# A graph network's last layer on one core: attention edges and node normalizations in one merged sweep

## What is computed

```python
xl = (x @ Wl + bl).reshape(n, H, C)
xr = (x @ Wr + br).reshape(n, H, C)
e = leaky_relu(xl[src] + xr[dst] + edge_attr @ We, 0.2)
logits = einsum('ehc,hc->eh', e, att)
alpha = softmax of logits over the edges with the same dst
out = segment_sum(alpha[..., None] * xl[src], dst) + bias
z1 = gelu(out) + x
out = layernorm(layernorm(z1) * gamma + beta + x)
```

## Time and profile before

| | us |
|---|---|
| time, median of 3 runs (15389.94 to 15460.77) | 15446.91 |
| span of the profiled execution | 14488.1 |
| of it `gat_edges`, first to last indirect DMA | 11556.0 to 13287.9 |
| of it `gat_nodes`, first addition to the end | 13304.7 to 14488.1 |
| busy in the span: VectorE, ScalarE, GpSimd, TensorE | 7705.7, 4873.1, 9282.4, 5851.2 |

### The profile page before, as it was taken

One profiled execution on the slowest core, in us unless ns is written; L12 is line 12 of the kernel. 1 busy time (PEld: TensorE's weight loads), 2 busy tenths in 40 slices (PEclk: granted clock), 3 DMA queues, 4 the chain that ended last, 5 costly groups with the idle time before them and its releaser, 6 DMA issues. The chain is left out here.

```text
span 14488.1 us, 162751 instructions
## 1 busy us (share of the span) xinstructions
PE 5851.2 (40%) x33264; PEld 4851.5 (33%) x33265; DVE 7705.7 (53%) x16353; ACT 4873.1 (34%) x8868; POOL 9282.4 (64%) x8791
## 2 busy tenths in 40 slices
PE   0000467356725660135634553455245455553000
PEld 0000356346625650024523452345244422221000
DVE  2200367346725679635535773355256544445898
ACT  0000123123312335434434552244146522223666
POOL 5767776577477633477657655774776377776665
PEclk9998678678867885577867776678577777776555
DMA  9201357357725777425624663355256611112333
GB/s 182 41 2 27 115 192 242 100 174 265 257 82 202 257 248 250 157 85 170 224 89 142 216 225 96 121 196 197 72 179 236 204 37 42 44 45 63 134 134 120
DMA packets 1063382, 2125.24 MB, mean 147 GB/s; under 512 B 264966, under 2 KB 576863, under 8 KB 1063288
## 3 DMA queue, kind: packets, MB, share of 16 engines
q1 hardware_dynamic: 421762, 1236.80, 25.6%
q10 hardware_dynamic: 403206, 512.24, 10.7%
q0 software_dynamic: 238336, 375.36, 9.0%
HBM read 1467.05 MB, written 719.11 MB: 151 GB/s over the span
## 5 line engine op out<-in xcount | busy, mean ns | idle before, releaser
L1304 POOL DMA_INDIRECT node_sums<-m_result,m_place x2744 | 3047.3, 1111 | 1027.3 <-issue 723.6
L1335 PE MATMUL m_turn<-k_ident,m_rows 128*128 128x128 f32 x2744 | 595.1, 387 | 2934.9 <-DMA m_rows<-node_rows_b,m_idx 1155.9
L1294 POOL DMA_INDIRECT m_rows<-node_rows_a,m_idx x1176 | 1268.2, 1078 | 471.1 <-issue 342.7
L1335 PEld LDWEIGHTS m_turn<-k_ident,m_rows 128*128 128x128 f32 x2744 | 466.5, 199 | 3036.6 <-issue 2125.7
L1294 POOL DMA_INDIRECT m_rows<-node_rows_b,m_idx x784 | 840.7, 1072 | 314.0 <-issue 224.8
L1391 PE MATMUL m_turn<-k_ident,m_in_y 128*128 128x128 f32 x5488 | 857.5, 302 | 404.3 <-ACT m_nodeT L1418 257.5
L1391 PEld LDWEIGHTS m_turn<-k_ident,m_in_y 128*128 128x128 f32 x5488 | 691.2, 156 | 532.6 <-ACT m_nodeT L1418 326.6
L1774 DVE SCALAR_TENSOR_TENSOR m_acc<-m_out,m_scales,m_res_b 128x128 f32<-128x128 f32 (+1 forms) x2352 | 634.7, 341 | 393.3 <-PE m_out L1403 322.9
L1403 PE MATMUL m_out<-k_sage_r,m_nodeT 128*128 128x128 f32 x3136 | 556.5, 351 | 584.7 <-DVE m_z L1886 571.2
L1761 DVE SCALAR_TENSOR_TENSOR m_res_b<-m_in_sums,m_scales,m_res_b 128x128 f32<-128x128 f32 (+1 forms) x2352 | 631.7, 342 | 292.3 <-DMA m_in_sums<-node_sums 292.0
L1418 ACT ACTIVATE m_nodeT<-m_turn 128x512 f32<-128x512 f32 x980 | 545.4, 596 | 701.4 <-PE m_turn L1391 697.6
(11 more groups left out here) (256 smaller groups left out, 17668.6 us busy)
## 6 DMA issues: line engine op xcount, KB each, us to landing
m_in_sums<-node_sums SPq DMA_DIRECT2D x679, 512.0 KB
m_in_y<-node_rows_a SPq DMA_DIRECT2D x291, 512.0 KB
node_rows_a<-m_y ACTq DMA_DIRECT2D x194, 512.0 KB
m_in_x<-in_x_dram SPq DMA_DIRECT2D x194, 512.0 KB
m_in_y<-node_rows_b SPq DMA_DIRECT2D x194, 512.0 KB
node_rows_a<-m_o ACTq DMA_DIRECT2D x194, 512.0 KB
m_w_all<-edge_w SPq DMA_DIRECT2D x147, 512.0 KB, 4.9
node_sums<-deg_zero ACTq DMA_DIRECT2D x98, 512.0 KB
```

Of the source, the lines that this page charges most:

```text
L1294: pool.indirect_dma_start(self.rows[b][:, t, :], None, self.table[:, :], bass.IndirectOffsetOnAxis(self.idx[b][:, t:t + 1], 0)).then_inc(s ...
L1304: pool.indirect_dma_start(self.dram["node_sums"][:, :], bass.IndirectOffsetOnAxis(self.place[b][:, t:t + 1], 0), self.result[b][:, t, :], ...
L1335: mm = pe.transpose(self.turn_ps[i % 2][:, n * P:(n + 1) * P], self.rows[i // 2][:, H * (i % 2) + n, :], self.k["ident"][:, :])
```

## The change

`gat_edges` and `gat_nodes` become one phase, `gat_conv` ("g8", tiles `g_...`): every engine walks a pair of edge chunks and then the node pairs that are ready (`edges_and_nodes`). The scatter goes to a table of its own, `gat_sums`, filled in the degrees phase with the layer's bias row instead of zeros (98 further DMAs of 512 KB behind the present ones); the rows of nodes with edges get the bias through `blb`, the bias of the values. So the addition L1118 goes. The product with gamma moves from GpSimd to VectorE. The addition of beta to x stays on GpSimd (`shift_x`), with a tile `xb` of its own for the result, and GpSimd walks the node pairs for it. The roots of both norms are taken by ScalarE (Sqrt) instead of Newton steps. Tiles have two copies, one for each chunk of a pair, and each chunk has its own norm tiles for 8 row slots. Waits with values of the loop counter are all kept positive by grants at the start.

```diff
+                dve.tensor_tensor(k["blb"][:, :], k["bl"][:, :], k["gat_bc"][:, :], ALU.add).then_inc(misc, 1)
...
+                act.wait_ge(constants_set, 4)
                 with act.Fori(0, sh.node_chunks) as c:
                     act.dma_start(dram["node_sums"][bass.ds(c * CH, CH), :].rearrange("(p j) f -> p j f", j=T),
                                   zero[:, :, :]).then_inc(zeroed, 16)
-                act.wait_ge(zeroed, 16 * sh.node_chunks)
+                with act.Fori(0, sh.node_chunks) as c:
+                    act.dma_start(dram["gat_sums"][bass.ds(c * CH, CH), :].rearrange("(p j) f -> p j f", j=T),
+                                  bias_rows[:, :, :]).then_inc(zeroed, 16)
+                act.wait_ge(zeroed, 2 * 16 * sh.node_chunks)
...
+                dve.tensor_copy(bias_rows[:, :, :], spread_slots(k["gat_b"][:, :], [P, T, D])).then_inc(constants_set, 1)
...
-        sweep(pool, sh.edge_chunks, sh.edge_chunks - 1, step)
-        for c in (sh.edge_chunks - 2, sh.edge_chunks - 1):
-            scatter(c, c % 2)
-        pool.wait_ge(self.scattered[0], 16 * T * ((sh.edge_chunks + 1) // 2))
-        pool.wait_ge(self.scattered[1], 16 * T * (sh.edge_chunks // 2))
+        def rest():
+            for c in (sh.edge_chunks - 2, sh.edge_chunks - 1):
+                scatter(c, c % 2)
+
+        edges_and_nodes(pool, k, sh, step, nodes, rest)
+        pool.wait_ge(self.scattered[0], self.all_scattered(0))
+        pool.wait_ge(self.scattered[1], self.all_scattered(1))
...
+    def load(self, sp, m, scattered_pairs):
+        ph, sh = self.ph, self.sh
+        for b in range(2):
+            c = m * 2 + b
+            sp.wait_ge(self.z1_done[b], m + 1)
+            sp.wait_ge(self.xb_done[b], m + 1)
+            sp.dma_start(self.x[b][0:sh.rows(c), :, :], node_rows(self.table, c, sh)).then_inc(self.x_in[b], 16)
+        for s in range(2):
+            sp.wait_ge(ph.scattered[s], ph.all_scattered(s) if scattered_pairs is None else scattered_pairs * (16 * T))
+            sp.sem_inc(ph.gate, 1)
+        for b in range(2):
+            c = m * 2 + b
+            sp.dma_start(self.sums[b][0:sh.rows(c), :, :], node_rows(self.sums_dram, c, sh)).then_inc(self.sums_in[b], 16)
+
+    def gelu(self, act, m):
+        for b in range(2):
+            n = self.sh.rows(m * 2 + b)
+            act.wait_ge(self.sums_in[b], 16 * m + 16)
+            act.activation(self.sums[b][0:n, :, :], self.sums[b][0:n, :, :], ACT.Gelu).then_inc(self.gelu_done[b], 1)
...
+    def scalar(self, act, m, scattered):
+        self.gelu(act, m)
+        self.norm2(act, m, 1, self.sh.rows((m - 1) * 2 + 1))
+        self.ln1[0].take_root(act, m, self.k["ln_eps"])
+        self.norm1(act, m, 0, self.ln1[1])
+        self.store_before(act, m)
+        self.norm1(act, m, 1)
+        self.ln2[0].take_root(act, m, self.k["ln_eps"])
+        self.norm2(act, m, 0, self.sh.rows(m * 2), self.ln2[1])
+        act.wait_ge(self.out_ready[0], m + 1)
+        self.store(act, m, 0)
...
+    def shift_x(self, pool, m, scattered):
+        for b in range(2):
+            n = self.sh.rows(m * 2 + b)
+            pool.wait_ge(self.x_in[b], 16 * m + 16)
+            pool.sem_inc(self.ph.gate, 1)
+            pool.wait_ge(self.z2_done[b], m + 1)
+            pool.tensor_tensor(self.xb[b][0:n, :, :], self.x[b][0:n, :, :], spread_slots(self.k["gat_beta"][0:n, :], [n, T, D]),
+                               ALU.add).then_inc(self.xb_done[b], 1)
...
+    def vector(self, dve, m, scattered):
+        n0, n1 = self.sh.rows(m * 2), self.sh.rows(m * 2 + 1)
+        one, two = self.ln1
+        self.add_x(dve, m, 0)
+        self.ln2[1].invert(dve, m)
+        self.add_x(dve, m, 1)
+        self.ln2[1].offset(dve, m)
+        dve.wait_ge(self.z1_done[0], m + 2)
+        one.take(dve, self.z1[0], n0, 0, 8)
+        one.part(dve, m)
+        dve.wait_ge(self.z1_done[1], m + 2)
+        two.take(dve, self.z1[1], n1, 0, 2)
+        one.square(dve, m)
+        two.take(dve, self.z1[1], n1, 2, 4)
+        one.variance(dve, m)
+        two.take(dve, self.z1[1], n1, 4, 8)
+        one.invert(dve, m)
+        two.part(dve, m)
+        one.offset(dve, m)
+        two.square(dve, m)
+        two.variance(dve, m)
+        two.invert(dve, m)
+        two.offset(dve, m)
+
+        one, two = self.ln2
+        self.mult_gamma(dve, m, 0)
+        self.add_xb(dve, m, 0)
+        dve.wait_ge(self.z2_done[0], m + 2)
+        one.take(dve, self.z2[0], n0, 0, 8)
+        self.mult_gamma(dve, m, 1)
+        one.part(dve, m)
+        self.add_xb(dve, m, 1)
+        one.square(dve, m)
+        dve.wait_ge(self.z2_done[1], m + 2)
+        two.take(dve, self.z2[1], n1, 0, 3)
+        one.variance(dve, m)
+        two.take(dve, self.z2[1], n1, 3, 8)
+        one.invert(dve, m)
+        two.part(dve, m)
+        one.offset(dve, m)
+        two.square(dve, m)
+        two.variance(dve, m)
+
+
+def edges_and_nodes(eng, k, sh, edge_step, node_unit, edges_end=None):
+
+
+    full, last = sh.edge_pairs, sh.node_pairs - 1
+
+    def ready(j):
+        at = slice(j + 1, j + 2) if isinstance(j, int) else bass.ds(j + 1, 1)
+        return eng.value_load(k["ready"][0:1, at], min_val=0, max_val=last)
+
+    def nodes(first, end, scattered):
+        with eng.If(first < end):
+            with eng.Fori(first, end) as m:
+                node_unit(m, scattered)
+        with eng.Else():
+            pass
+
+    def edges(j):
+        for b in range(2):
+            edge_step(2 * j + b, b, j)
+
+    edges(0)
+    edges(1)
+    nodes(ready(0), ready(1), 1)
+    with eng.Fori(2, full) as j:
+        edges(j)
+        nodes(ready(j - 1), ready(j), j)
+    edge_step(2 * full, 0, full)
+    if edges_end:
+        edges_end()
+    nodes(ready(full - 1), last, None)
+    node_unit(last, None)
...
-                        act.activation(val[h][:, :], val_ps[:, :], ACT.Identity, bias=k["bl"][:, 0:1]).then_inc(val_set, 1)
+                        act.activation(val[h][:, :], val_ps[:, :], ACT.Identity, bias=k["blb"][:, 0:1]).then_inc(val_set, 1)
...
-        gat_edges(nc, a, k, dram, sh, "e8", rows_b)
-        gat_nodes(nc, k, dram, sh, "n8", rows_b, out)
+        gat_conv(nc, a, k, dram, sh, "g8", rows_b, out)
```

More of the change, by code:

```diff
@@ L636, in gat_edges, with gat_conv @@
+def gat_conv(nc, a, k, dram, sh, name, table, out):
     n_attr = a["edge_attr_16"].shape[1]
@@ L642, in chunk_before @@
         return c - 1, 1 - b, q - (1 - b)
-    with EdgePhase(nc, name, k, dram, sh, table, both_ends=True) as ph:
+    with EdgePhase(nc, name, k, dram["gat_sums"], sh, table, both_ends=True) as ph:
+        nodes = GatNodes(ph, k, dram, sh, table, out)
         attr = [ph.sb(f"attr{b}", [P, T, n_attr]) for b in range(2)]
```

278 lines of the change are left out of this document (148 added, 130 removed).

## The result

The changed kernel took **15616.26 us** (median of 4 runs, 15558.47 to 15700.16), the kernel before, run beside it, 15418.42 us (15312.71 to 15460.77). The ratio is **1.0152, 95% interval 1.0112 to 1.0192**: slower, by 198 us between the medians, by 173 to 296 us by the interval. The prediction said 15600 and +153. That the number came out is in part luck: it was summed from a trace of a level at which the change costs 31 to 44 us, and compared with runs of another level, in which waits that this trace doesn't hold add the rest.

The account below looks back on a forecast made before the run. GpSimd paced the edges, nobody alone the nodes; merged, the ScalarE and VectorE chain would bind. Layer terms of 3059 against 2933 us (+126) plus 27 gave +153; with 959 above the span, 15600 us (+1.0%), range 15430 to 15780.

Parts of the forecast that it names:

- 43 units in groups: Node pairs following edge pairs 4 to 23 in the merged layer: 24 x 31.0 + 19 x 28.5 = 1286 us.
- The bound moved from GpSimd to the chain of ScalarE and VectorE: Merged layer: GpSimd no longer sets the pace; the ScalarE and VectorE chain, edges then nodes, does.
- Degrees phase, +27: 98 more writes of 512 KB in the degrees phase cost 27 us; below 0, above 60.
- The unit, 28.5 and 31.0: One node pair in the new order: 28.5 us, or 31.0 us where GpSimd's addition overlaps it.
- Table switch: ScalarE's table change in a node unit: 1.30 us by the trace; a documented drain would make it about 2.66.
- rival E: A table switch stops ScalarE longer than its load: 125 us more, 15725, or 15735 by the page; chance 0.08.
- Edge pair, 62: Two edge chunks in the merged order, with branches and Exp's table load, take 62 us, 58 to 64.
- GpSimd's margins, 7 and 3 us: After a node group, the next edge pair's first gather is hidden by 7 us, the second by under 3.
- The sign that it named: Merged stretch: GpSimd waits on VectorE's `z2` some 14 times for 26 us and more.
- Rival D: The 7 and 3 us margins are missing: 5 to 10 us per edge pair, 100 to 200 more, 15750; chance 0.16.
- Rival C: Edge chain restarts at once, GpSimd stays the bound: layer 2950 us, 15491, no measurable change; chance 0.18.
- The median above the span: Whole kernel: the median lies 959 us above the profiled span of 14488.1, left as it is and added.

Follow-up runs that it names:

- second trace of after: Changed kernel run again unchanged, beside the kernel before on the same chip: 14520.4 us, ratio 1.0018 to the kernel before; its layer took 2953 us.
- lower level: Sets of runs in which the unchanged kernel before took 14484 and 14489 us; the changed kernel measured 1.0018 and 1.0025 there.
- upper level: Sets of runs in which the unchanged kernel before took 15390, 15418 and 15802 us; the result's 1.0152 was measured at 15418.
- the two runs with five more products: Five extra TensorE matrix products ahead of each second half's transposes: kernel before 14482.9 us, ratio 0.999; changed kernel 14709.2 us, ratio 1.0147.
- the set at 15802: Runs beside the kernel before at 15802.2 us; kernel before with biases folded and product with gamma on VectorE took 15621.1 us, ratio 0.9887.

## Why the prediction was right, and where it was not

The layer, first gather to the end, term by term in us, with the second trace of after (lower level) and the trace of the result (upper level). Edge pairs are the distance from the first addition of the first group to the end of the last group's last unit, less 43 units.

| term | predicted | lower level | upper level |
|---|---|---|---|
| start to the first addition | 285 + 62 = 347 | 352 | 382 |
| 43 units in groups | 1286 | 1264 | 1264 |
| 19 further edge pairs | 19 x 62 = 1178 | 1109 | 1304 |
| chunk 48 | 59 | 50 | 50 |
| last units | 189 | 178 | 178 |
| layer | 3059 | 2953 | 3179 |
| degrees phase | +27 | 0 | 0 |

Set against the level of the trace that it was read from, the sum is 133 us too high (3086 against 2953): it said +153, and +31 to +44 came. It lies 45 us from the measured +198 because the compared runs were of the upper level, where late signals add more than the sum had too much. No term of it stands for them. So the number is in part luck, while the mechanism below is not.

- **The bound moved from GpSimd to the chain of ScalarE and VectorE**: shown, by the two runs with five more products. It is the core of the prediction, and it is why the changed kernel loses more where TensorE's signals are late.
- **Degrees phase, +27**: wrong, though its stated lower bound, 0, named this case. First gathers of the first convolution start at 1296.7, 1284.7 and 1286.2 us in the three traces of the changed kernel, 1293.6 and 1283.9 in the two of before. The step that failed is the comparison of two windows: it took the slower first window for the price of any write. The new ones go out from 361.0 to 612.3 us, and TensorE did more transposes beside them (184 in 280 us) than without them in before (176).
- **The unit, 28.5 and 31.0**: 29.4 us overlapped, 29.3 at the end, 28.1 without GpSimd's additions. The 1264 us count the last unit of each group as 29.4 too, though it has no next addition to be measured by; an error there would lie in the edge pairs. The mechanism was right in detail (product and variance held back by GpSimd, 0.7 and 1.6 us), the size by 1.6 us too large where it overlaps, as VectorE's delay reaches ScalarE only in part.
- **Table switch**: the trace of after repeats: 1.28 us of load and the next instruction 1.29 to 1.30 us after the load's start, so the forecast's 1.30 us stands. No drain of its own shows; by the unit's length rival E is out, but the runs meant to take the loads away did not.
- **Edge pair, 62**: the term that was mis-sized, in both directions. At the lower level 58.4, just inside its 58 to 64. ScalarE is free 23.5 us into a last unit (its first addition at 13637.6, its last scaling ends at 13661.2), so 5.9 us before a next unit could start, not 2.4. The rest of the working holds: first copy 2.4 us later, two chunks 61.4 instead of 62.5. At the upper level 68.6, outside them, by late signals that no row of the trace of before could show.
- **GpSimd's margins, 7 and 3 us**: right. In the second trace of after the rows of a first chunk are turned at 13801.7 and copied from 13809.9, those of the second turned at 13836.6 and copied from 13838.7: 8 and 2 us. The sign that it named came as well: 14 waits of 26 us and more for `z2`, at either level. At the lower level the run without these waits and without GpSimd's additions is 19 us shorter in all. At the upper level the late copies stand behind just these waits, and what they cost there was not tested. Rival D's waiting for gathered rows happens (21 times), but ScalarE waits only 47.2 us in all for turned rows in that stretch.
- **Rival C** named 2950 us for the layer (its own terms add up to 2944), 3 us from the lower level's value, on another ground: GpSimd is not the bound there (58.4 us of edges per pair is less than its 69.4). A close figure is no proof of its reason.
- **The median above the span**: wrong in its ground. It was no constant to add but the sign that the trace and the times belong to different levels, and with it what the sum could not hold. (Small slips beside it: the 2933 us of before begin 1.3 us ahead of the first gather, and 1664 is 49 times the gathers and 46 times the scatters.)

What the change is made of, from the runs at the lower level: folding the biases gives -214 us; the units in the written order, each behind the other, cost 14734 - 14270 = +464; interleaving them with the edges gives -214. These are steps from one version to the next across two sets of runs whose before differs by 5 us, so that they add up (+36, against +31 measured within one set) confirms nothing. The +464 hold several edits that were not taken apart: the written order of the unit, two copies of each tile instead of four, the root on ScalarE with its table loads, gamma on VectorE; the last alone is worth -18 in the old order. I had compared the new unit with 24.2 us; the right partner was 19.9, and the gain of the biases was hidden in the loss of the units.

At the upper level the merged layer pays 3179 - 2953 = 226 us for late signals, the old edge stretch some 103 (in the set at 15802). The difference, 123, and the 31 us from below are 154 of the 198 measured between the medians (the interval begins at 173). What the rest is stays open, since no trace of before exists at 15418. Open too is why TensorE's signals come late at all. The runs show that it goes with the set of runs, touches stages that no version changes, and that in the result's merged stretch the gathers of the next chunk were under way in all 14 late cases and hardly in the five that are not late: in seven of the 14 the copy starts 2.4 to 3.2 us after the last of the sixteen, in the others earlier. No run moved the gathers away at the upper level, so that they cause it is not shown.

Of all versions the one with folded biases in the old order is the best measured, 0.9877; the one with the product with gamma moved is another 18 us shorter by its node stretch.

## What to carry to other kernels

Replacing a stretch that is bound by one engine with a merged chain can take away the cover of what this engine hid: test it by putting a few microseconds of delay into another engine of both versions. Take a bundle of edits apart before judging it; here one edit alone gained 214 us, the interleaving as much, and the rewritten unit lost more than both. And set a profile's span beside the times it is compared with: if they differ by per cents, the trace is of another condition.

## What the runs showed of the hardware

- One kernel took 14484 and 14489 us in two sets of runs and 15390 to 15802 in three others, each set on one chip and spread by 1.3% at most. In the result's trace (upper level) the copy of a second half starts up to 13.6 us after the start of the last transpose's record; in the traces of the lower level 0.31 us.
- Wide GpSimd instructions hold up small VectorE ones: without 98 additions of some 2.3 us, 225 us in all, VectorE's busy time was 258 us shorter (three groups of the root's steps of 192 ns had stood at 776, 582 and 510 on average).
- 98 more writes of 512 KB in the degrees phase cost nothing that shows (the first gather behind them within 3 us), at a DMA share of 0.87 and 216 GB/s:

```profile
400.00:680.00 280.00, 22.58 (x184) 21.26 (x184) 85.09 (x89) 0.00 (x0) 207.16 (x195) 1.00 0.87 216
```
- Table loads stayed where Copy or Identity took Gelu's place, though the row scalings use Identity beside Sqrt without one.
